# Delta rule on Trainium2: decays from a scan, keys scaled on ScalarE, query norm in the gating, sums of squares over four quarters

## What is computed

```python
q = l2norm(silu(conv(x @ Wq)));  k = l2norm(silu(conv(x @ Wk)));  v = silu(conv(x @ Wv))
def step(S, inp):
    qt, kt, vt, gt, bt = inp
    S = S * jnp.exp(gt)
    delta = (vt - kt @ S) * bt
    S = S + kt[:, None] * delta[None, :]
    return (S, qt @ S)
o_n = o * jax.lax.rsqrt(jnp.mean(o * o, axis=-1, keepdims=True) + NORM_EPS) * norm_w
o_n = o_n * jax.nn.silu(gg)
```

## Time and profile before

| | us |
|---|---|
| median of 3 runs (1919.13 to 1927.75) | 1920.87 |
| profiled execution | 1922.77 |
| its span, first to last instruction | 1920.8 |
| delta-rule stage in that span, about | 826 to 1656 |

### The profile page before, as it was taken

How to read it: one execution, slowest core, us unless ns; L and a number is a source line. 1 busy time by engine, 2 the same in 40 slices (tenths; PEclk the granted TensorE clock), 3 DMA queues, 4 the chain that set the end, 5 groups by cost and what they waited for, 6 DMA issues and landing times. The chain is left out here.

```text
span 1920.8 us, 27888 instructions
## 1 busy us (share of the span) xinstructions
PE 1557.3 (81%) x10666; PEld 1029.1 (54%) x10666; DVE 1038.3 (54%) x2369; ACT 666.4 (35%) x1185; POOL 694.9 (36%) x1097
## 2 busy tenths in 40 slices
PE   4787787887959996757799999999999996488782
PEld 3354544544436663323566666656665675365562
DVE  3856556455124543736467566766667642145652
ACT  3062251531512222544344544454444521022112
POOL 3020110300000000017768676777668763111343
PEclk8999899898979997889899999999999986598997
DMA  1000000000030003230231223222321121421355
GB/s 54 1 1 2 23 1 1 23 1 1 12 90 15 31 12 124 82 50 17 39 56 26 42 45 56 39 40 34 56 50 29 30 38 28 125 84 66 79 119 138
DMA packets 216902, 84.33 MB, mean 44 GB/s; under 512 B 166265, under 2 KB 211682, under 8 KB 216770
## 3 DMA queue, kind: packets, MB, share of 16 engines
q1 hardware_dynamic: 205330, 68.10, 15.8%
q0 software_dynamic: 5376, 12.59, 2.5%
q10 hardware_dynamic: 6064, 1.86, 0.4%
HBM read 50.80 MB, written 31.72 MB: 43 GB/s over the span
## 5 line engine op out<-in xcount | busy, mean ns | idle before, releaser
L1810 DVE SCALAR_TENSOR_TENSOR d_conv<-d_prep,k_cw,d_conv 128x511 f32<-128x511 f32 (+2 forms) x288 | 214.2, 745 | 33.0 <-ACT d_conv L1641 26.3
L1762 POOL TENSOR_TENSOR d_prod<-d_blk 64x30 f32<-64x30 f32 (+4 forms) x360 | 172.9, 480 | 102.4 <-DMA d_blk<-mid_a_blk 75.1
L1427 PE MATMUL d_prep<-k_hT,k_w 128*128 128x512 f32 x384 | 190.9, 622 | 22.0 <-POOL d_power L1736 12.7
L1766 POOL TENSOR_TENSOR d_blk<-d_blk,d_prod 64x30 f32<-64x30 f32 (+4 forms) x360 | 184.2, 512 | 28.2
L424 ACT ACTIVATE a_probs<-a_acc 128x896 f32<-128x896 f32 x128 | 117.1, 918 | 173.2 <-PE a_acc L248 110.6
L523 DVE TENSOR_REDUCE a_top<-a_turn 128x4 f32<-128x512 f32 (+3 forms) x240 | 147.6, 652 | 49.0 <-PE a_turn L210 40.5
L471 POOL TENSOR_TENSOR a_rstd<-a_rstd,a_mhalf 128x4 f32<-128x4 f32 x4 | 4.1, 1027 | 369.6 <-DVE a_rstd L575 369.6
L1427 PEld LDWEIGHTS d_prep<-k_hT,k_w 128*128 128x128 f32 x384 | 68.6, 198 | 83.4 <-issue 48.9
L1641 ACT ACTIVATE d_conv<-d_prep,k_cw 128x512 f32<-128x512 f32 x96 | 65.9, 686 | 134.1 <-PE d_prep L1427 133.6
L1466 PE MATMUL d_prep<-d_kq 128*128 128x256 f32 x384 | 93.8, 388 | 15.0 <-DVE d_qkT L1842 15.0
L1466 PEld LDWEIGHTS d_prep<-d_kq 128*128 128x128 f32 x384 | 72.2, 195 | 43.6 <-DVE d_qkT L1842 26.8
(11 more groups left out here) (356 smaller groups left out, 3576.0 us busy)
## 6 DMA issues: line engine op xcount, KB each, us to landing
mid_gate<-p_gate SPq DMA_DIRECT2D x4, 768.0 KB, 3.4
mid_v<-p_v_tok SPq DMA_DIRECT2D x4, 768.0 KB, 3.7
d_v_h<-mid_v SPq DMA_DIRECT2D x12, 256.0 KB, 5.5
d_gate_h<-mid_gate SPq DMA_DIRECT2D x12, 256.0 KB, 5.4
mid_a_blk<-d_AT SPq DMA_DIRECT2D x48, 64.0 KB, 2.0
d_blk<-mid_a_blk SPq DMA_DIRECT2D x12, 256.0 KB, 3.6
mid_u_blk<-d_blk SPq DMA_DIRECT2D x12, 256.0 KB, 2.9
mid_l_blk<-d_blkT SPq DMA_DIRECT2D x12, 256.0 KB, 3.7
```

What stands on the lines that cost most here:

```text
L1427: last = nc.tensor.matmul(PB[f % 2][:], w[:, n % 2, i, k, :], hT[:, k, b * T:(b + 1) * T], start=k == 0, stop=k == CK - 1)
L1762: nc.gpsimd.tensor_tensor(pr, blk[:, 0:t, t:t + 1].broadcast_to([lanes, t, m]), blk[:, t:t + 1, t + 1:BLK].broadcast_to([lanes, t, m]), AL ...
L1766: nc.gpsimd.tensor_tensor(blk[:, 0:t, t + 1:BLK], blk[:, 0:t, t + 1:BLK], pr, ALU.subtract).then_inc(subst, 1)
L1810: ins = nc.vector.scalar_tensor_tensor(dst, PB[f % 2][:, 0:T - j], cw[:, n % 2, f % 2, TAPS - 1 - j:TAPS - j], dst, ALU.mult, ALU.add)
```

## The change

It does five things. (1) The decay matrix is no longer made from differences. The projections write exp(g) per token to a DRAM tensor `alpha`, with 0 for the first token of each chunk; the delta rule loads a head's 4 x 512 values to all 128 partitions (`load_decays`, four DMAs behind `spread_blocks` on SP) and four `tensor_tensor_scan` instructions on VectorE (`scan_decays`) turn them in place into the decays, with a constant `diag`. For heads 2 and up they stand in `recur` behind the first R, for heads 0 and 1 in `turn`. `spread`, `differences`, `decay_up` and their constants go. (2) `keep_keys` moves from VectorE to ScalarE, one activation per tile with a scale from SBUF. (3) The query's norm is no longer applied to o; eps is scaled by it instead (`eps_q`), and GpSimd's power has half its width. (4) `sum_squares` is called for two batches at a time. (5) Orders change: on TensorE `level2_x` calls alternate with the last four `correlate` calls, and the transpose of the last output goes ahead of the second sums; on ScalarE the last `keep_out` goes ahead of the last `silu`; on VectorE the eight `weigh` calls run through and `scale_values` goes ahead of `finish`; gates get two buffers and their own load.

The core of the diff:

```diff
+            def load_decays(n):
+                if n:
+                    sp.wait_ge(attn, 8 * n)
+                for b in range(BATCH):
+                    sp.dma_start(alpha[:, b, :], alpha_d[n:n + 1, b, :].broadcast_to([P, T])).then_inc(alpha_in[b], 16)
...
                 if n + 2 < D_H:
                     spread_blocks(n + 2)
+                if n + 3 < D_H:
+                    load_decays(n + 3)
                 store(n)
...
-            def sum_squares(n, b):
-                if b == 0 and n:
-                    pe.wait_ge(n_half, 2 * n)
-                if b == 2:
-                    pe.wait_ge(n_half, 2 * n + 1)
-                pe.wait_ge(squared, BATCH * n + b + 1)
+            def sum_squares(n, half):
+                if n or half:
+                    pe.wait_ge(n_half, 2 * n + half)
+                pe.wait_ge(squared, BATCH * n + 2 * half + 2)
...
             def turn(m, q):
-                if q < D_H:
-                    differences(q, 0)
                 if 0 <= m < D_H:
                     turn_keys(m, ORDER[:3])
-                if q < D_H:
-                    sum_squares(q, 2)
-                    sum_squares(q, 3)
                 if 1 <= m:
                     turn_out(m - 1, CH - 1)
+                if q < D_H:
+                    sum_squares(q, 1)
...
                     turn_sums(q, 1)
-                    for b in range(1, BATCH):
-                        differences(q, b)
-                        correlate(q, 2 * b)
-                        correlate(q, 2 * b + 1)
+                    correlate(q, 2)
+                    correlate(q, 3)
+                for i in range(BATCH):
+                    if q < D_H:
+                        correlate(q, 4 + i)
+                    if 0 <= m < D_H:
+                        level2_x(m, i)
                 if 0 <= m < D_H:
-                    for i in range(BATCH):
-                        level2_x(m, i)
                     for i in range(BATCH):
                         level2_l(m, i)
...
+            def keep_keys(n, i):
+                b = ORDER[i]
+                act.wait_ge(k_turned, BATCH * n + i + 1)
+                for c in range(CH):
+                    t = b * CH + c
+                    ins = nc.scalar.activation(k_tok[:, t, :], LB[b][:, c, :], ACT.Copy, scale=decays[:, 1, n, t:t + 1])
+                ins.then_inc(k_ready, 1)
...
+            def scan_decays(n):
+                for b in range(BATCH):
+                    dve.wait_ge(alpha_in[b], 16 * n + 16)
+                    nc.vector.tensor_tensor_scan(alpha[:, b, :], alpha[:, b, :], diag[:], 0.0, ALU.mult, ALU.add).then_inc(decayed, 1)
...
                         nc.vector.tensor_copy(R[:], r_src).then_inc(r_ready, 1)
+                    if ahead and c == 0:
+                        scan_decays(n + 2)
                     dve.wait_ge(solved, CH * n + c + 1)
...
-                nc.vector.tensor_tensor(o[:], o[:], vec(norm[:, n % 2, 1, :]), ALU.mult).then_inc(rchain, 1)
...
                 if q < D_H:
+                    if q < 2:
+                        scan_decays(q)
                     take_sums(q, 1)
                     scales(q)
-                    for f in range(4):
+                    for f in range(8):
                         weigh(q, f)
-                if invert:
-                    keep_keys(m, 0, 2)
```

More of the change, by code:

```diff
@@ L951, in delta_constants @@
     out["c_after"] = (i[:, None] > i[None, :]).astype(np.float32)
-    out["c_past"] = in_bf16(np.repeat(np.where(i[:, None] <= i[None, :], 0.0, NEG)[:, None, :], CH, 1))
+    out["c_diag"] = np.tile(np.eye(P, dtype=np.float32), (1, CH))
     return out
@@ L1114, in _ @@
             for lhsT, bank, at in ((upto, GB[0], 0), (after, GB[0], n), (ones, GB[1], 0)):
-                last = nc.tensor.matmul(bank[:, at:at + n], lhsT[:], g[:].rearrange("p h t -> p (h t)"), start=True, stop=True)
+                nc.tensor.matmul(bank[:, at:at + n], lhsT[:], g[:].rearrange("p h t -> p (h t)"), start=True, stop=True)
+            for a in range(2):
+                last = nc.tensor.transpose(GB[1][0:n // 2, 2 * P + a * P:2 * P + (a + 1) * P],
+                                           g[:].rearrange("p h t -> p (h t)")[:, a * (n // 2):(a + 1) * (n // 2)], ident[:])
             last.then_inc(summed, 1)
@@ L1342, in layer1_delta_rule @@
         w_in, v_in = [sem(f"w_in{n}") for n in range(2)], [sem(f"v_in{n}") for n in range(3)]
+        gate_in, alpha_in = [sem(f"gate_in{n}") for n in range(2)], [sem(f"alpha_in{b}") for b in range(BATCH)]
         carrier, sp_carrier = sem("carrier"), sem("sp_carrier")
@@ L1394, in store @@
                 sp.dma_start(o_d[n, :, :, :], o_out[:]).then_inc(stored, 16)
+            load_decays(0)
             for n in range(3):
                 load_values(n)
+            for n in range(2):
+                load_gate(n)
             spread_blocks(0)
+            load_decays(1)
             load_weights(2)
@@ L1401, in _ @@
             spread_blocks(1)
+            load_decays(2)
             for n in range(D_H):
@@ L1674, in recur @@
                         convolve(n + 2, 2 * c + 1)
-                keep_out(n, CH - 1)
+                if not ahead:
+                    keep_out(n, CH - 1)
             def prepare(n):
@@ L1849, in scale_values @@
                 dve.wait_ge(nchain, 2 * n + 2)
-            def keep_keys(n, start, end):
-                for i in range(start, end):
-                    b = ORDER[i]
-                    dve.wait_ge(k_turned, BATCH * n + i + 1)
-                    dec = decays[:, 1, n, b * CH:(b + 1) * CH]
-                    nc.vector.tensor_tensor(k_tok[:, rows[b], :], LB[b][:], dec[:, :, None].broadcast_to([P, CH, P]), ALU.mult).then_inc(k_ready, 1)
             def keep_l(n, i):
```

170 lines of the change are left out of this document (68 added, 102 removed).

## The result

The changed kernel takes 1979.12 us in the median (1972.38 to 1984.07), against 1921.03 of the kernel before beside it: 1.0294 times as long, 95% interval 1.0251 to 1.0337. The profiled execution is the fastest of its runs, 1972.38 us with a span of 1970.3.

The account below looks back on a forecast made before the run. GpSimd's closed loop was to bound the kernel: 61.2 + 3.9 (scans) + 0.8 (`gate_out`) + 0.8 (low clock) = 66.7 us a head. Ten heads from 943.8 end at 1610.8, +58 us in all: 1979 us, range 1916 to 2000.

Parts of the forecast that it names:

- The loop: Delta-rule chain where one head's inversion waits on the previous one's: 61.2 us, with added terms 66.7 us a head.
- Blocks out: From a head's last `weigh`, diagonal blocks go to DRAM and back until GpSimd starts: 7.15 us.
- Substitution: GpSimd's `substitute` of the diagonal blocks: 37.5 us, plus 3.9 for scans and 0.8 for `gate_out`.
- Blocks back: From the end of `substitute` to the matmuls that need the inverse: 10.0 us.
- `level2_x` to W: From `level2_x` 0 to W, the end of a head's last `weigh`: 6.5 us, plus 0.8 for low clock.
- The scans: Four VectorE scans of 1.23 us hold up GpSimd beside them: 3.9 us more for `substitute`.
- Rival 3: The decay row loads land late: at 22 us a head is 75 us and the time 2060; chance 0.06.
- gate_out: Its two remaining products fall into the end of `substitute`: +0.8 us a head, ends 0 and 1.4.
- The first head: First `substitute` starts 1.8 us later and scans add 3.9; the last `weigh` of head 1 ends at 943.8.
- TensorE's own path: TensorE's time per delta-rule head apart from the loop: 60 us instead of 62.2, plus about 1.
- Rival 1: Scans beside `substitute` cost GpSimd nothing: loop 61.2 us, about 1917 us, not slower; chance 0.20.
- What would show it: Trace signs: heads 65 to 68 us apart, TensorE idle some 5 before `level2_x`, GpSimd's sum up 3 to 5.

Follow-up runs that it names:

- e1: Changed kernel with all eight `correlate` calls of the next head put before the first `level2_x` on TensorE; 1911.75 us, 0.9950 of the kernel before.
- e4: e1 with each head's four scans moved from the recurrence to the turn, ahead of the last sums; 1907.93 us, 0.9924 of the kernel before.
- e7: Changed kernel, its TensorE order kept, with only the scans moved from the recurrence to the turn; 1947.17 us, 1.0127 of the kernel before.
- e3: e1 with each scan replaced by an in-place multiplication by 1.0, decay recurrence left out; 1899.76 us, 0.9881 of the kernel before.
- e2: Changed kernel with each scan replaced by an in-place multiplication by 1.0, decay recurrence left out; 1952.25 us, 1.0131 of the kernel before.
- e8: e1 with `correlate` 0 and 1 moved ahead of the joined sums of squares; 1904.83 us, 0.9910 of the kernel before.
- e10: Changed kernel, its alternating order kept, with `correlate` 0 and 1 moved ahead of the joined sums; 1989.24 us, 1.0362 of the kernel before.
- e11: e10 with sixteen more matmuls a head, results overwritten, ahead of TensorE's wait for the inverted blocks; 1976.07 us, 1.0281 of the kernel before.
- e5: Kernel before with only `correlate` 4 to 7 alternating with the `level2_x` calls; 1937.76 us, 1.0082 of the kernel before.

## Why the prediction was right, point by point

**The loop** was the right bound, and each leg came near its term. Blocks out: predicted 7.15, measured 7.40. Substitution: 42.2, measured 41.31. Blocks back: 10.0, measured 10.26. `level2_x` to W with its low clock: 7.3, measured 7.07. Sum: 66.7, measured 66.04. W(1) was forecast for 943.8 and came at 941.49, W(11) for 1610.8 and came at 1601.81. So against its own measure, the profiled execution, the sum is 8.4 us too long (1980.8 against 1972.38); that it meets the median so closely is luck of that size, since the changed kernel's runs spread over 12 us.

**The scans.** The estimate of 1.23 us was near: 1.20 with no GpSimd instruction beside it (three scans of head 0), 1.25 in the rows above beside GpSimd (1.32 in the mean of the page). The price for the substitution, 3.9, was 3.5 (e1 against e4), nearest to the value taken among its ends of 0, 1.8 and 4.9. In the rows above GpSimd's four instructions lost 0.80 to 0.85 us each (1.12 to 1.27 instead of 0.32 to 0.47), about two thirds of a scan. The reason is in their starts and ends. The first scan ended at 1084.48; the GpSimd instruction began at 1083.47, 0.24 after the scan, and ended at 1084.59, 0.11 after its end, though it needs 0.32. So it stood still until the scan had ended, but for 0.21 us. All 44 GpSimd instructions that the scans of this run stretched lost the time from their start to the scan's end, less 0.17 to 0.22 us. That is near the 0.24 that the prediction had read from the earlier trace rows.

By the rule of the Trainium skill's page "SBUF — State Buffer" (Who interferes with whom) the engine that starts first keeps the ports that the two share for its whole instruction and the other is fully blocked. The trace agrees with it to those 0.2 us. What the prediction made of the rule, a loss of the scan's whole length, was too much, because the blocked instruction began 0.05 to 0.60 us after the scan.

The row loads landed when the blocks did, as said: GpSimd began at 1082.08, the first scan at 1083.23. Rival 3 did not arise. eps came 1.5 us behind the end of its matmuls (1087.09), and 1.3 to 2.9 us in heads 0 to 9, where about 1 was allowed.

Two sums of the prediction slipped. 4 x (1.23 - 0.24) is 4.0, where it has 3.9. With all upper ends a head is 61.2 + 4.9 + 1.4 + 2.5 = 70.0 us and the time some 2013; its 69.4 and 2007 take `gate_out` at 0.8. Neither moves the forecast by more than 1 us.

**gate_out** in the end of the substitution was forecast at +0.8. With the scans moved, e4 has 37.9 against 37.6, +0.3, and e7, whose loop is closed, 38.3 to 38.5 in most heads, +0.8.

**The first head.** Here two terms were off and partly cancel. The first substitution was to start 1.8 us later; it started 0.4 earlier (881.23, before 881.63). Its lengthening by 3.3 was foretold as 3.9. `level2_x` of head 0 therefore comes 2.9 us later than in the earlier trace rows, not 5.7. The low clock behind it I had right: 9.46 to W, forecast 9.0.

**TensorE's own path** is the step that failed. I forecast 60 us a head plus about 1, some 5 us of waiting at every `level2_x`, and 0.8 us for the low clock. Measured: 64.7 to 64.9 where there is no wait, and a mean wait of 1.4 us over ten heads. At full clock the path is shorter than I thought: e3's undisturbed heads take 58.1. One cause is that the joined sums cost nothing: eight matmuls take 1.06 us, as four did in the earlier trace rows, where I had added 1.0. But the clock was mis-sized by far, 58 us lost over ten heads instead of some 8. Since TensorE would otherwise have waited for the blocks, most of that did not lengthen the head; it ate the wait. From GpSimd's end to `level2_x` it is 10.26 on average, where 10.0 is needed when TensorE is ready, so this cost 0.3 us a head at most. What counts in full is what falls between `level2_x` and W, and that mean of 0.6 (7.07 against 6.4 to 6.5) is close to the 0.8. The sum came out right with a wrong picture of TensorE beside it.

**Rival 1's time was too low.** With no contention the loop was to be 61.2 and the time 1917. e2, with less contention, took 1952, and e7, with the scans moved, 1947. W of head 1 came at 937.07 and 939.21 there, near the rival's 937.4, so the difference lies in the heads: 64.9 and 63.8 us. In e2 the substitution has 1.5 us more than the rival's 37.5, and 1.8 us more lie between `level2_x` and W, where the low clock comes back behind the wait. In e7 it is 1.6 in the substitution, of which three heads with scans beside it have the most, 0.5 on the way back of the blocks and 0.3 between `level2_x` and W. The range's lower end rested on that price.

**What would show it**: heads 65 to 68 us apart held for six of eleven, from `level2_x` to `level2_x`; the first is 70.0, and four lie between 64.3 and 64.9; the substitution's 3 to 5 us more beside the scans held; no table load is left in these heads. A wait of some 5 us ahead of every `level2_x` did not.

## What to carry to other kernels

When an edit reorders one engine's queue, ask whether the wait it moves now stands between a slow engine's result and that same engine's next input: spare time that was 5.9 us with the chain open is gone once it is closed, and from then on each microsecond on any leg is paid in every round (moving the scans is worth 32 us here, and 4 with the chain open). Put the work that starts the next round ahead of the wait for the last one. With the old order kept, the rest of this change makes the kernel faster by 0.5% (e1), 0.8% with its scans away from the substitution (e4), and 0.9% with `correlate` ahead of the sums (e8); the intervals of the three overlap.

## What the hardware showed that I had not expected

- A wait of TensorE can cost more than its own length. After 4.86 us of standing still, the granted clock was 0.70 on the way to W and 6.4 us of work took 9.1. Sixteen useless matmuls in such a place made e10 13 us faster (e11). The length of the wait alone does not tell: a wait of 1.94 us in e2 was followed by a granted clock of 0.79 (8.18 us to W), one of 1.97 us in e5 by 1.00 (7.59 us).
- Also where no DMA is waited for, the new turn's idle times of 2.6 and 1.9 us were followed by low stretches in some heads and not in others: in e3, with the same instructions, a turn's window has a clock of 0.77 in one head and 1.00 in another. What decides between the two stays open.

```profile
1092.30:1104.30 12.00, 9.76 (x48) 1.00 0.49 88
1150.80:1165.70 14.90, 12.81 (x49) 0.77 0.40 72
```

- VectorE and GpSimd took turns in SBUF, row by row. A GpSimd instruction of 0.3 to 0.5 us that began beside a scan ended 0.2 us short of its own length after the scan. Four scans cost the substitution 3.5 us; four 128x512 multiplications of 0.43 us in their place cost it about 0.5, though they took turns as well.
- Eight matmuls of the sums (512 columns in, 32 partitions out) into four quarters of a bank's partitions take 1.06 us, four into two quarters 1.05.
